# Wide attention: the values' tails as one block-masked 128-wide matmul, and the second batch's values and the output-bias product moved into the prologue

## The reference, cut to what matters

```python
q = (query @ Wq + bq).reshape(b, sq, 16, 64)
k = (key @ Wk + bk).reshape(b, 154, 16, 64)
v = (value @ Wv + bv).reshape(b, 154, 16, 64)
scores = jnp.einsum('bqhd,bkhd->bhqk', q, k) / 8.0
attn = jax.nn.softmax(scores, axis=-1)
out = jnp.einsum('bhqk,bkhd->bqhd', attn, v).reshape(b, sq, 1024)
out = out @ Wo + bo + residual
# then a layer norm with gamma and beta, gated and added to x
```

## Time and profile before

| | us |
|---|---|
| median of 3 runs | 1831.9 |
| lowest, highest | 1828.62, 1832.82 |
| the profiled execution, its own time | 1827.25 |
| its span | 1825.5 |
| PE busy in the span | 1467.0 (80%) |
| VectorE (DVE) busy | 1062.0 (58%) |
| ScalarE (ACT) busy | 685.4 (38%) |
| GpSimd (POOL) busy | 394.5 (22%) |
| granted TensorE clock, mean | 0.886 of full speed |

### The profile page before, as it was taken

One profiled execution on the slowest core, in us unless ns is written; L12 is line 12 of the kernel. 1 busy time (PEld: TensorE's weight loads), 2 busy tenths in 40 slices (PEclk: granted clock), 3 DMA queues, 4 the chain that ended last, 5 costly groups with the idle time before them and its releaser, 6 DMA issues. The chain is left out here.

```text
span 1825.5 us, 27092 instructions
## 1 busy us (share of the span) xinstructions
PE 1467.0 (80%) x9994; PEld 875.0 (48%) x9994; DVE 1062.0 (58%) x2645; ACT 685.4 (38%) x1824; POOL 394.5 (22%) x488
## 2 busy tenths in 40 slices
PE   3677835679999979995888588898887968887997
PEld 3333414545555546664333355565554543344564
DVE  6545541254556656555453576676675864555886
ACT  3223412256656422223333365455552133433111
POOL 1000042244323300000100277667651001000000
PEclk8777867889999989996898799999989977988999
DMA  2430011140000000001000000000000010000000
GB/s 48 146 115 14 9 42 56 37 102 13 1 1 1 1 1 1 1 1 22 7 9 2 1 1 1 1 1 1 1 1 1 1 21 8 9 1 1 1 1 24
DMA packets 46824, 32.18 MB, mean 18 GB/s; under 512 B 16076, under 2 KB 41109, under 8 KB 46693
## 3 DMA queue, kind: packets, MB, share of 16 engines
q1 hardware_dynamic: 42885, 25.43, 5.5%
q0 software_dynamic: 2048, 4.20, 1.0%
q10 hardware_dynamic: 1760, 0.82, 0.2%
HBM read 19.80 MB, written 5.77 MB: 14 GB/s over the span
## 5 line engine op out<-in xcount | busy, mean ns | idle before, releaser
L2628 ACT ACTIVATE L2a_pr<-psum,L2a_negmax 128x512 f32<-128x512 f32 (+3 forms) x256 | 131.9, 526 | 128.2 <-DVE L2a_negmax L2698 70.1
L536 ACT ACTIVATE L1x_praw<-psum,L1x_negmax 128x154 f32<-128x154 f32 x256 | 96.2, 390 | 82.6 <-DVE L1x_negmax L621 82.3
L2496 PE MATMUL psum<-ident,L2a_pr 128*128 128x128 f32 x640 | 89.6, 286 | 34.0 <-DVE L2a_pT L2718 20.1
L311 POOL TENSOR_TENSOR L1x_pm<-L1x_praw,L1x_total 128x1024 f32<-128x1024 f32 x32 | 60.7, 1897 | 159.5 <-DVE L1x_total L627 103.3
L1452 DVE TENSOR_REDUCE L0x_negmax<-psum 128x6 f32<-128x924 f32 (+1 forms) x48 | 47.7, 1011 | 80.6 <-PE psum L1026 77.6
L2496 PEld LDWEIGHTS psum<-ident,L2a_pr 128*128 128x128 f32 x640 | 74.8, 147 | 41.1 <-issue 23.5
L1452 DVE TENSOR_REDUCE L2x_negmax<-psum 128x6 f32<-128x924 f32 (+1 forms) x48 | 47.8, 1012 | 74.1 <-PE psum L1026 57.9
L1452 DVE TENSOR_REDUCE L3x_negmax<-psum 128x6 f32<-128x924 f32 (+1 forms) x48 | 47.8, 1011 | 68.9 <-PE psum L1026 57.6
L1813 ACT ACTIVATE L1f_sg<-psum 128x512 f32<-128x512 f32 x64 | 38.2, 597 | 121.8 <-PE psum L1765 121.8
L621 DVE TENSOR_REDUCE L1x_negmax<-psum 128x4 f32<-128x616 f32 x64 | 50.8, 795 | 45.3 <-PE psum L358 45.0
L1874 DVE SCALAR_TENSOR_TENSOR L3f_acc<-psum,L3f_comb,L3f_acc 128x128 f32<-128x128 f32 x256 | 71.9, 344 | 8.3 <-PE psum L1778 5.0
(11 more groups left out here) (649 smaller groups left out, 3563.2 us busy)
## 6 DMA issues: line engine op xcount, KB each, us to landing
expert_arena<-in_L_ffn_w SPq DMA_DIRECT2D x16, 256.0 KB, 5.8
L1f_gu<-in_L_ffn_gate_up_w SPq DMA_DIRECT2D x8, 256.0 KB, 3.9
slots_in<-zero SPq DMA_DIRECT2D x1, 1280.0 KB, 9.2
L0f_xs<-slots_in SPq DMA_DIRECT2D x5, 256.0 KB, 3.7
resid<-in_x SPq DMA_DIRECT2D x4, 256.0 KB, 5.7
L1f_dn<-in_L_ffn_down_w SPq DMA_DIRECT2D x8, 128.0 KB, 4.0
slots_out<-L0f_ys SPq DMA_DIRECT2D x16, 64.0 KB, 1.6
expert_arena<-in_L_ffn_w_gate_up SPq DMA_DIRECT2D x2, 512.0 KB, 5.9
```

The source lines that it names most:

```text
L311: nc.gpsimd.tensor_tensor(pm[:, n % 2].rearrange("p j t k -> p (j t) k"), praw[:, n % 3, :, :, 0:MAIN].rearrange("p j t k -> p (j t) k"), ...
L536: nc.scalar.activation(praw[:, n % 3, j, t, :], psum[:, 2 * u + j, x * CTX:(x + 1) * CTX], ACT.Exp, bias=negmax[:, n % 2, u, j, x:x + 1], ...
L2496: last = nc.tensor.transpose(psum[:, TURN + n // 4, n % 4 * P:(n % 4 + 1) * P], pr[:, m % RING, n * P:(n + 1) * P], core.ident[:])
L2628: ins = nc.scalar.activation(pr[:, i % RING, SEQ * j + lo:SEQ * j + hi], psum[:, bank + j, lo:hi], ACT.Exp, bias=negmax[:, i % RING, e:e + ...
```

## The change

Three edits, all in `wide_attention`. First, the tail's two matmuls of 32 rows by 64 columns for each trip become one of 128 rows by 128 columns over all of `tT`, added into all of bank OV; so that a head meets only its own block of rows, `vt` is zeroed outside it: the copy that evicts a tail value becomes a multiply by `core.quad`, spread over the 64 columns of a head. Second, the four value matmuls of batch 1 and their evictions move from trips 4, 6, 8 and 9 to the prologue, into banks 0 to 3, behind the values of batch 0. Third, the product bv x Wo and the bias sum move from behind the queries to behind the values of batch 0. The values of batches 2 and 3 stay where they are. On VectorE the bias sum and the four evictions of batch 1 now stand ahead of the sum of batch 0's gathered rows.

```diff
--- before.py
+++ after.py
@@ -388,12 +388,8 @@
                         pe.wait_ge(s["o"], m)
                     for j in range(G):
                         h = G * g + j
-                        nc.tensor.matmul(psum[DK * j:DK * j + DK, OV, :], vm[:, b % 2, h * DK:(h + 1) * DK], pT[:, m % 3, j, :], start=True, stop=False)
-                    for j in range(G):
-                        h = G * g + j
-                        rows = slice(32 * (h % 4), 32 * (h % 4) + 32)
-                        last = nc.tensor.matmul(psum[DK * j:DK * j + DK, OV, :], vt[rows, b % 2, h * DK:(h + 1) * DK], tT[rows, :], start=False, stop=True)
-                    last.then_inc(s["pv"], 1)
+                        nc.tensor.matmul(psum[DK * j:DK * j + DK, OV, :], vm[:, b % 2, h * DK:(h + 1) * DK], pT[:, m % 3, j, :], start=True, stop=True)
+                    nc.tensor.matmul(psum[:, OV, :], vt[:, b % 2, g * P:(g + 1) * P], tT[:], start=False, stop=True, skip_group_check=True).then_inc(s["pv"], 1)
 
                 def output(m):
 
@@ -417,18 +413,24 @@
                     keys(0, i, i)
                 for i in range(4):
                     value(0, i, 3 + i)
+                for g in range(NG):
+                    last = nc.tensor.matmul(psum[0:1, OUT, 0:D], w["bv"][:, g:g + 1], w["wo"][:, g * P:(g + 1) * P], start=(g == 0), stop=(g == NG - 1))
+                last.then_inc(s["bo_ps"], 1)
+                for i in range(4):
+                    if i < 3:
+                        pe.wait_ge(s["k"], i + 1)
+                    else:
+                        pe.wait_ge(s["v"], 1)
+                    value(1, i, i)
+                pe.wait_ge(s["bo"], 1)
                 rowsT(0, OUT)
                 for g in range(NG):
-                    if g < 3:
-                        pe.wait_ge(s["k"], g + 1)
+                    if g < 4:
+                        pe.wait_ge(s["v"], 5 + g)
                     elif g < 7:
                         pe.wait_ge(s["v"], g - 2)
                     query(g, g)
                 pe.wait_ge(s["q"], NG)
-                for g in range(NG):
-                    last = nc.tensor.matmul(psum[0:1, OUT, 0:D], w["bv"][:, g:g + 1], w["wo"][:, g * P:(g + 1) * P], start=(g == 0), stop=(g == NG - 1))
-                last.then_inc(s["bo_ps"], 1)
-                pe.wait_ge(s["bo"], 1)
 
                 for n in range(NS + 5):
                     b, g = n // NG, n % NG
@@ -486,10 +488,10 @@
                             pe.wait_ge(s["pt"], 2 * (n - 2) + 2)
                         if n >= 3 and n % 2:
                             pe.wait_ge(s["tt"], (n - 1) // 2)
-                        if b and g in (0, 1):
+                        if b >= 2 and g in (0, 1):
                             value(b, 2 + g, H1)
                         if b + 1 < B:
-                            if g in (4, 6):
+                            if b and g in (4, 6):
                                 value(b + 1, g // 2 - 2, H1)
                             if g in (2, 5, 7):
                                 keys(b + 1, (2, 5, 7).index(g), H1)
@@ -612,7 +614,13 @@
                     dve.wait_ge(s["v_ps"], 4 * b + i + 1)
                     if b >= 2 and i == 0:
                         dve.wait_ge(s["pv"], NG * (b - 1))
-                    nc.vector.tensor_copy((vm if i < 2 else vt)[:, b % 2, (i % 2) * 512:(i % 2 + 1) * 512], psum[:, bank, :]).then_inc(s["v"], 1)
+                    cols = slice((i % 2) * 512, (i % 2 + 1) * 512)
+                    if i < 2:
+                        nc.vector.tensor_copy(vm[:, b % 2, cols], psum[:, bank, :]).then_inc(s["v"], 1)
+                    else:
+                        nc.vector.tensor_tensor(vt[:, b % 2, cols].rearrange("p (x c e) -> p x c e", x=2, c=4),
+                                                psum[:, bank, :].rearrange("p (x c e) -> p x c e", x=2, c=4),
+                                                core.quad[:].unsqueeze(1).unsqueeze(3).to_broadcast([P, 2, 4, DK]), ALU.mult).then_inc(s["v"], 1)
 
                 def maxima(n, u):
                     if n >= 2 and u == 0:
@@ -667,12 +675,14 @@
 
                 for i in range(4):
                     value(0, i, 3 + i)
+                dve.wait_ge(s["bo_ps"], 1)
+                nc.vector.tensor_tensor(bo[:], psum[0:1, OUT, 0:D], w["bo"][:], ALU.add).then_inc(s["bo"], 1)
+                for i in range(4):
+                    value(1, i, i)
                 summed(0)
                 normed(0)
                 summed(1)
                 normed(1)
-                dve.wait_ge(s["bo_ps"], 1)
-                nc.vector.tensor_tensor(bo[:], psum[0:1, OUT, 0:D], w["bo"][:], ALU.add).then_inc(s["bo"], 1)
                 for n in range(NS + 5):
                     b, g = n // NG, n % NG
                     if n < NS:
@@ -686,9 +696,9 @@
                     if n >= 3 and n % 2 and n - 2 < NS:
                         tails(n - 2)
                     if n < NS:
-                        if b and g in (0, 1):
+                        if b >= 2 and g in (0, 1):
                             value(b, 2 + g, H1)
-                        if b + 1 < B and g in (4, 6):
+                        if b and b + 1 < B and g in (4, 6):
                             value(b + 1, g // 2 - 2, H1)
                     if b and g == 5:
                         finished(b - 1, 0)
```

## The result

The changed kernel takes 1824.83 us in the median of 15 runs (1818.26 to 1829.26), the kernel before 1829.53 us in 15 runs beside it (1821.28 to 1833.0). The medians lie 4.7 us apart. The ratio is 0.9967 with a 95% interval of [0.9953, 0.998], so it is faster by 0.33% or 6.0 us; in a later set of 12 runs (after_again3, 1823.15 against 1830.57) the ratio was 0.9956 [0.9939, 0.9974], 8.0 us. The forecast was -7.5 us and 1824.4. Of the change's three parts two can be read to a hundredth of a microsecond, and the third, the prologue, holds what the prediction did not foresee.

The account below looks back on a forecast made before the run. PE was taken to bound the loop, DVE's order the prologue. Terms -4.0 - 3.5 + 0 = -7.5 us took the profiled 1827.25 to 1819.7 and the median 1831.9 to 1824.4, range 1820 to 1829.5.

Parts of the forecast that it names:

- Part 1: Loop tails as one 128-wide matmul: 0.15 us gained in each of 27 trips, -4.0 us.
- The five trips that were counted out: Loop trips 8, 12, 16, 32 and 33, where another chain ends last; no gain expected from the full-width tail.
- Rival 1: Full-width tail gains nothing and the prologue loses up to 1 us: 1829 us; chance 0.15.
- Rival 4: Array drains on both sides of the loop's tail: slower, +8.3 us, giving 1840; chance 0.05.
- 0.26 us: Loop tail's possible extra per trip: waiting out the main passes, then loading weights in the open (0.19 us).
- Part 2: Second batch's values leave loop trips 4, 6, 8 and 9: 0.95 + 3 x 0.86, -3.5 us.
- Rival 3: Freed value passes in the loop turn into waits for ACT's query evictions: +3.0 us, 1827.4; chance 0.07.
- Part 3: Prologue with moved bias product, sum and four values: counted at 0, bounds -1.4 and +2.3 us.
- first sum: DVE's sum of the first batch's gathered rows in the prologue, expected 2.45 us later, at 361.1.
- the 0.3 us from an earlier return of the clock: Prologue queries run slow for a shorter time at 1.2 GHz; 0.3 us taken back.
- DVE evicts each about 0.2 us behind its end: Prologue: each moved value's eviction follows its matmul by about 0.2 us, the last from 360.5 to 361.1.
- Rival 2: Prologue evictions ahead of the first batch's sum cost their 2.3 us in full: 1826.7 us; chance 0.15.

Follow-up runs that it names:

- after_again3: The changed kernel, unchanged, traced again and timed in 12 runs: 1823.15 us against 1830.57 before, ratio 0.9956.
- tail_only: Kernel before with only the full-width tail matmul and masked eviction; values, bias product and sum unmoved: 1823.98 us against 1830.04, ratio 0.998.
- prologue_only: Kernel before with only the second batch's values, bias product and sum moved to the prologue; old tails and copies: 1825.58 us against 1830.04, ratio 0.999.
- bias_only: Kernel before with only the bias product and sum moved ahead of the first sum of gathered rows: 1831.18 us in one execution, against 1830.57.
- before: The kernel before the change, its first trace: profiled execution 1827.25 us; median of 15 runs 1829.53 us.
- after_again2: The changed kernel, unchanged, for a further trace: 1820.03 us, with the kernel before at 1824.59 us beside it.
- before_again1: The kernel before the change, unchanged, for a second trace: 1824.23 us.
- after: The changed kernel with all its parts, its first trace: profiled execution 1822.82 us; median of 15 runs 1824.83 us.
- nogather2: Changed kernel again without 16 of 24 gathers, their rows cleared, late loads waiting for the last query eviction: 1817.51 us.
- after_nogather: Changed kernel without 16 of 24 gathers, rows cleared instead, late loads waiting for the last query eviction: 1806.4 us.
- act_evicts: Changed kernel with ScalarE instead of DVE evicting the second batch's four values in the prologue: ratio 0.9983 to the kernel before.

## Why the prediction was right, and where it was not

**Bound.** The loop is PE's: PE stayed at 55.80 of 60 us, and what was taken from its queue came off the time. 6.97 of the 7.5 us came.

**Part 1, -4.0 forecast, -3.45 measured.** The size in a trip was right: 0.15 us where a query follows the tail. The term that was too large is the count. The five trips that were counted out are flat (8, 12, 16, 32, 33). The rest were priced alike, though in the last batch (trips 24 on) no query follows the tail. Where values, the gate's or the output matmuls follow, the gain is 0.15 us all the same (24, 28, 30, 34). Trip 35, priced too, lies outside the intervals and gives 0.1 us at most. Where four short transposes follow, the gain is 0.10 (26, 27, 29, 31): in trip 27 the transposes start 1.00 us behind the tail before and 0.96 now. In trip 25 they start 1.2 us behind it in either version, and nothing is gained. 21 x 0.146 + 4 x 0.10 = 3.5, not 27 x 0.15. The price of following 64-wide work sits where it was put: the tail takes 0.97 us, the 0.86 of a full-width matmul and 0.1 for coming behind 64-wide work, and the query behind it 0.85. Rival 1 has fallen with this, since tail_only is faster with an interval that ends below 1. The section Overview of TensorEngine Tiling (Array Packing), a page of the Trainium skill, speaks of up to twice the speed where a dimension is 64 or less. The upper bound was not reached here: the two pairs took 1.01 us where the full-width matmul takes 0.86. Rival 4 has fallen as well: the main values take 1.01 us to the next start as before, and the tail 0.97, so no 0.26 us are lost on either side.

**Part 2, -3.5 forecast, -3.51 measured.** 0.95 + 3 x 0.86 was the sum; 0.88, 0.86, 0.86 and 0.90 were found. In trip 4 the query's step to the next start grows from 0.96 to 1.06 us once the scores stand right behind it (prologue_only), and the scores' step shrinks from 0.90 to 0.85, so the value gave 0.88 there, not 0.95. Trip 9 gave 0.90 where 0.86 was expected, which makes good about half of that; the total is closer than its terms. The wait of 0.32 us for a query's eviction in the rows above is trip 4's, ahead of its values, and was there before (0.33). Rival 3, freed passes that turn into waits, has fallen: PE's waits from trip 4 on are those of before.

**Part 3, 0 forecast.** Where handovers are prompt, its steps came as written: first sum +2.2 us (+2.45 forecast), transposes 368.09 (367.7, from a first key product 0.56 us later), normalisation 1.11 us beside no clearing (1.1 forecast), and the maxima +0.1 us in the mean of the three traces of before, where -0.2 was forecast. One term went the other way: the queries took 10.03 us and not less than 9.91, so the 0.3 us from an earlier return of the clock did not come: it came back at 375.8, 5.9 us into the queries.

Two things were missing. The first is small: trips 0 to 3, which the prediction put at nothing. From the first maxima to trip 4's scores it takes 23.65 to 23.72 us in every version with the product moved, bias_only among them, and 22.63 to 23.33 where it stays. The query of trip 0 starts 4.43 to 4.45 us behind the first maxima, and what it costs depends on when the granted clock falls. PE in before, after_again2 and tail_only:

```profile
386.08 1.73 PE L334 MATMUL psum<-L1x_xnT,projections 128*128 128x512 f32 x2 [3.39 <-ACT L1x_xnT L513]
387.74 2.35 PE L358 MATMUL psum<-L1x_kT,L1x_qT 64*128 64x154 f32 x16
...
386.52 2.07 PE L334 MATMUL psum<-L1x_xnT,projections 128*128 128x512 f32 x2 [3.64 <-ACT L1x_xnT L515]
388.52 2.43 PE L358 MATMUL psum<-L1x_kT,L1x_qT 64*128 64x154 f32 x16
...
392.51 1.13 PE L334 MATMUL psum<-L1x_xnT,projections 128*128 128x512 f32 x2 [3.39 <-ACT L1x_xnT L509]
393.56 2.34 PE L358 MATMUL psum<-L1x_kT,L1x_qT 64*128 64x154 f32 x16
```

From start to start that query takes 1.05 us in tail_only, where the clock falls to 0.5 at 393.7, behind it; 1.66 in before (fall at 386.5) and 1.26 in before_again1, where it falls in its midst; and 2.00 in after_again2, where it fell at 386.1, ahead of it. The stretch to trip 4's scores follows: 22.63, 23.33, 22.92 and 23.72 us. So the cost comes by way of the clock. In the four traces with the product in its old place the fall comes 4.8 to 5.6 us behind the first maxima, in the ten with the product moved 4.0 us behind them or earlier. That is +0.6 us against the mean of before (23.08), given back behind the point at which the prediction stopped reading. That it comes with the product's move is shown; why the fall comes earlier then, with PE idle where the product had been, is argued.

The second is large where it occurs: the late handovers, 5 to 6 us of prologue in the changed kernel. The step that failed in those traces is "DVE evicts each about 0.2 us behind its end". It was read from a trace in which all handovers were prompt. But they are not the change's price in particular, since tail_only has 40.98 us with the old prologue. Rival 2 (the evictions ahead of the first sum cost their 2.3 us in full) is refuted in prompt executions, where the end of the prologue moved by 0.1 us. In late ones it stays open, as no trace of the kernel before is of that kind. The timed runs speak against a price of 5 us that the changed kernel alone would pay: it would be left with 1 us or so of its gain, a ratio above 0.999, and both intervals end below that (0.998 and 0.9974). Either the timed executions are prompt, or both kernels pay alike.

**Sum.** Loop -6.97, trips 0 to 3 +0.6, prologue +0.1: -6.3 us, against -6.0 and -8.0 us timed. The forecast of -7.5 was 1.2 us too good, 0.5 of it in the count of trips, 0.6 in trips 0 to 3. The forecast of 1824.4 came so close by luck: it was added to 1831.9, the median of three runs, and the median of 15 runs before is 1829.53. That start was 2.4 us too high, and it cancelled most of the 2.8 us by which the forecast gain exceeds the 4.7 between the medians.

## What to carry to other kernels

Where an engine is over 90% busy in a stretch, price an edit by the distance between starts on it, and count the trips by what follows the edited step: the gain of this tail was 0.15 us in front of a query, 0.10 in front of short transposes and nothing in front of a wait. Follow a moved step past the stretch that it left; the cost here lay in the trips behind the prologue. And look at more than one profiled execution of both kernels before you believe a stage that hangs on many handovers, and compare how many records they hold: the first pair differed by 5.8 us in a prologue that turned out equal.

## What was not expected of the hardware

**Late handovers.** In the prologue, between 355 and 385 us, POOL issues gathers. In eight traces engines there began 0.4 to 4.2 us after their input and they themselves were ready, several times by 2.1 or 2.8; VectorE and ScalarE above all, TensorE once by 0.7. In the others they began 0.15 us after at most. Kernels that were traced in one set were of one kind, save for the one without 16 gathers, which had one late step only; both kinds were met on the same chip. So the gathers may have to do with it, but in that run the late loads were moved too, and what decides between the kinds is not settled.

The recording itself is a rival that no run tests. The late traces lack records: 3546 to 3611 landings of DMAs, against 4176 to 4182 in the prompt ones with all gathers, though the packets are as many; of the 384 landings of the layer's 24 gathers, after holds 92 and after_again2 all. nogather2, with its one late step, holds 3701 where after_nogather holds 3926. So what the late traces name as having ended an idle time ("remote", "issue") can't be relied on, and the timed executions may not have the lateness at all: the profiled execution of tail_only was the slowest of its 12 and that of prologue_only the slowest of its 12 by 10 us, but that of act_evicts, late too, was the fastest of its 12.

**The clock in a full stretch.** In prologue_only the granted clock (the column behind POOL's) fell to 0.5 at 613.9 us, in the midst of work:

```profile
612.00:614.00 2.00, 2.00 (x17) 1.88 (x18) 1.04 (x6) 0.58 (x3) 0.00 (x0) 0.98 0.01 4
614.00:616.00 2.00, 2.00 (x12) 1.46 (x11) 0.29 (x2) 0.00 (x0) 0.00 (x0) 0.50 0.00 0
...
624.00:626.00 2.00, 1.90 (x8) 1.74 (x8) 1.86 (x12) 0.00 (x0) 0.00 (x0) 0.54 0.00 0
```

PE had been busy since 605.73 us, when its last wait, of 0.83 us, ended. It stayed at 1.2 GHz for 6.8 us and fell once more at 624.2 for 3.4, right behind a wait of 1.47 us; the two trips took 2.42 and 2.29 us longer for it. No other trace shows a fall at this place; the nearest is one of 3.4 us at 608.7 in tail_only, which cost it 1.57. The others come in trip 16, behind the 2.6 us in which PE waits for the transposed rows: they cost 1.4 to 1.7 us in seven traces, 3.0 in one and nothing in the other six. So the loop of one execution can differ by up to 6.4 us from another's with no instruction changed, and the comparison by intervals is the way around it.
